# Attention entry of a fused attention and mixture-of-experts kernel: three waits for one, scores placed ahead of the ranks, and batch 0's copies on ScalarE

## The chip, the cores and the metric

One core of one Trainium2 chip. The metric is the device time of one launch in microseconds, as the median over runs of the same kernel. The profile is one further execution of it.

## The reference, cut to what matters

For x of 16 batches x 512 tokens x 128 features in float32 the result is x + attention(layernorm(x)) + experts(layernorm(x)):

```python
xn = (x - mean) / sqrt(var + 1e-5)
# attention: 16 heads of 8, causal
q, k, v = heads(xn @ Wq), heads(xn @ Wk), heads(xn @ Wv)
q, k = q / norm(q), k / norm(k)
o = softmax(where(causal, 8.0 * q @ k.T, -max)) @ v
attn = merge(o) @ Wo
# experts: 8 of 128 -> 512 -> 128, each token to its best two
probs = softmax(xn @ Wr.T)
top_v, top_i = top_k(probs, 2); top_v /= sum(top_v)
ffn = sum over e of (gelu(xn @ W1[e].T + b1[e]) @ W2[e].T + b2[e]) * weight_e
```

## The kernel before

**Stages.** Stage A (`stage_a`) goes through the 16 batches in pairs: LayerNorm on VectorE (DVE), transposes and the joint product with the router, q and k weights on TensorE (PE), squares, norms and copies on ScalarE (ACT), sums of squares on GpSimd (POOL). Then comes the entry of attention, which is what is changed. `attention` then runs batches 0 to 7, then the experts' tiles (`between`), then batches 8 to 15.

**The routing at the entry.** DVE picks the two best experts of each token in quarters (`select`, L1105); the last quarter is done after stage A. PE sums the picks (L985), DVE copies the sums (L1273, `totals`), PE multiplies them again (L992, L994, semaphore `counted`), and DVE works out from the counts where each expert's rows begin (L1280 to L1310). That gives `pad_at`: POOL fills the padding of the slots from a block of zeros with an indirect DMA (`pad_last_tiles`, L623, 128 rows of 8 KB; semaphore `padded`). PE gives each token its rank within its expert (L997 and L999, into PSUM bank 7, semaphore `placed`), DVE turns ranks into slot numbers (L1320 to L1328), clears the bank `ps_o` (L1331) and raises `routed`.

**A batch of attention.** It has 12 units of scores, each for three of the (side, half, head group) pieces of `PIECES`. PE computes a unit into one of two halves of six PSUM banks (`scores`, L892), ACT takes the exponential of the 1,536 columns (L812), POOL clears what is above the diagonal (`mask`, L664, one or two instructions a unit), and PE multiplies the probabilities with the values in ten chunks (`weigh`, L926) into `ps_o`. `scores` of unit k waits for the exponential of unit k-2; a chunk waits for the masks of all its units. Chunks 0 to 4 make the first half of a batch: DVE transposes it out of `ps_o` (`evacuate`, L1355), and chunk 5 waits for that (`o_evac`). Chunk 3 wants the masks up to unit 5, chunk 4 those up to unit 6, chunk 6 up to unit 8, chunk 7 up to unit 9.

**Preparing the next batch.** Between the units PE makes the next batch's four tiles of q, k and v (`project`, L870; each waits until the tile before it is out of bank 7, `proj_evac`). DVE scales q and k (L1222), copies the values out (L1229), splits q and k into two half precision parts (L1238, L1240) and doubles them (L1245, L1246, `dup_done`). SP then issues a DMA transpose of that tile into `qks` (`turn_qk`, L431). `scores(b, par, 0)` waits for all four transposes of its batch (`qk_turned`). Batch 0's four tiles are projected ahead of the routing (L978 on), each in a bank of its own. POOL's queue in batch 0 also carries eight indirect moves of token rows to their slots (`move`, L650). They stand between the masks of units 5 to 10, and ahead of the first of them, behind the mask of unit 5, POOL waits for `routed` and `padded`:

```python
order = [[], [], [], [], [], [0], [1, 2], [3], [4, 5], [6], [7], []]   # moves behind each unit's mask
```

Each engine carries out its own queue in the order of the program. In batch 0 PE's order is: scores 0 to 3, project(1,0), scores 4, weigh 0, scores 5, project(1,1), weigh 1, scores 6, weigh 2, scores 7, project(1,2), weigh 3, scores 8, project(1,3), scores 9, weigh 4, scores 10, weigh 5 and 6, scores 11, weigh 7, and then scores(1,0). DVE's order is share_values(0), the four `prepare` of batch 1, `pick_tiles`, `evacuate(0, 0)`, `divide`, share_values(1).

Of the kernel before, what the change touches and what calls it, by code (L numbers as in the profile page):

```python
# [29 lines left out]
def build(nc, x, Wq, Wk, Wv, Wo, Wr, W1, b1, W2_, b2, out):  # L30
# [68 lines left out]
    with ExitStack() as ctx:  # L99
# [154 lines left out]
        routed = sem("routed")  # L254
# [279 lines left out]
        def _(pool):  # L534
# [141 lines left out]
            def body(b, par, second=False, last=False):  # L676
# [3 lines left out]
                if known(b, 0):  # L680
                    pad_last_tiles()
                for k in range(UN):
                    mask(b, k)
                    if known(b, 0) and k == 5:
                        pool.wait_ge(routed, 1)
                        pool.wait_ge(padded, 16)
# [59 lines left out]
        def _(act):  # L746
# [28 lines left out]

            def step(i, par, j):
# [21 lines left out]
            stage_a(act, step)  # L798
            for s in range(2):
                squares(NB // 2 - 1, 1, s)  # L800
            for i in range(NB // 2 - 3, NB // 2):
                roots(i)
# [31 lines left out]
        def _(pe):  # L834
# [35 lines left out]
            def project(b, i):  # L870
# [4 lines left out]
                if not known(b, 0):  # L875
                    if i == 0 and known(b, 1):
                        pe.wait_ge(routed, 1)
# [48 lines left out]
            def weigh(b, par, c):  # L926
# [3 lines left out]
                if c == 0:  # L930
                    pe.wait_ge(proj_evac, TB * (b + 1))
                    if known(b, 0):
                        pe.wait_ge(routed, 1)
# [47 lines left out]

            pe.wait_ge(selected, T // ST)
# [13 lines left out]
            mm.then_inc(counted, 1)  # L996
            pe.matmul(ps_pc, before[:], flat_both, start=True, stop=False)  # L997
# [4 lines left out]
            pe.wait_ge(bt_ready, 1)  # L1002
            pe.wait_ge(proj_evac, TB)

            def body(b, par, second=False, last=False):
# [3 lines left out]
                fresh = known(b, 0) or known(b, HALF)  # L1009
                for k in range(UN):  # L1010
                    scores(b, par, k)
                    if k == 1 and not last and not known(b, 0):
# [3 lines left out]
                    elif k == 3:  # L1016
                        if not fresh:
                            weigh(b - 1, 1 - par, 9)
                        if not last:
                            project(b + 1, 0 if known(b, 0) else 1)  # L1020
                    elif k == 4:
                        weigh(b, par, 0)
                    elif k == 5:
                        if not last:
                            project(b + 1, 1 if known(b, 0) else 2)
# [3 lines left out]
                    elif k == 7:  # L1029
                        if not last:  # L1030
                            project(b + 1, 2 if known(b, 0) else 3)
                        weigh(b, par, 3)
                    elif k == 8 and known(b, 0):
                        project(b + 1, 3)
# [4 lines left out]
                    elif k == 9:  # L1039
# [4 lines left out]
                        if not known(b, 0):  # L1044
                            out_project(b - 1, TB * (b + 1) if last else TB * (b + 2))
# [53 lines left out]
        def _(dve):  # L1099
# [110 lines left out]
            def unload(b, par, i, late=False):  # L1210
# [5 lines left out]
                if some(tile):  # L1216
# [6 lines left out]
                    .then_inc(qn_done, 1)  # L1223
                if some(CN * (b - 2)):
# [6 lines left out]
            def halve(b, i):  # L1231
# [3 lines left out]
                if some(b):  # L1235
# [5 lines left out]
                    .then_inc(lo_done, 1)  # L1241
                dve.wait_ge(lo_done, tile + 1)
# [24 lines left out]
            for c in range(TOPK):  # L1267
                select(T // ST - 1, c)
            dve.wait_ge(btr_done, 1)
            dve.tensor_copy(wexp[:, :, B1C:W2C], psum[:, 5, 0:E * MC].rearrange("p (e c) -> p e c", e=E))\  # L1270
                .then_inc(bt_ready, 1)
            dve.wait_ge(counted, 1)
# [316 lines left out]
```

## Time and profile before

| what | value |
|---|---|
| median of three runs | 680.27 us (679.78 to 681.35) |
| the profiled execution's own time | 680.41 us |
| its span | 678.7 us |
| mean granted clock of TensorE | 0.975 |
| PE busy | 615.8 us (91%) |
| DVE busy | 465.7 us (69%) |
| ACT busy | 449.9 us (66%) |
| POOL busy | 418.0 us (62%) |
| mean DMA rate | 132 GB/s |

The busy times are sums over one execution. They say that PE is the engine with the least idle time; where its idle time lies has to be read from the stretches. Times of the timeline and of the windows are microseconds from the start of the span. A row of the timeline gives start, duration, engine, line, operation and names, and in square brackets how long the engine had been idle and what the profile holds responsible.

### The profile page before, as it was taken

How to read it: one execution, taken by the hardware profiler on the slowest of the kernel's cores; microseconds unless marked ns; L12 is line 12 of the kernel's file. 1: busy time of each engine (PE TensorE's matmuls, PEld its weight loads, DVE VectorE, ACT ScalarE, POOL GpSimd, SP SyncE). 2: the span in 40 equal slices, each digit the busy share in tenths (PEclk: the TensorE clock that was granted, in tenths of full speed). 3: DMA queues.
4: the chain of work that ended last, by engine and by line, in shares of the span. 5: the costliest groups of instructions: out<-in, count | busy, mean ns of one | idle time of the engine just before them, and what ended most of it. 6: DMA issues, size and time to landing. Idle time of an engine off the chain costs nothing. (4 is left out here: it accounts for less than half of the span.)

```text
span 678.7 us, 21454 instructions
## 1 busy us (share of the span) xinstructions
PE 615.8 (91%) x7417; PEld 411.7 (61%) x7417; DVE 465.7 (69%) x1312; ACT 449.9 (66%) x689; POOL 418.0 (62%) x584
## 2 busy tenths in 40 slices
PE   2877558999999999999999999999999999999965
PEld 2755323444444438999999999999984444444423
DVE  7799986766676776445545446777566687878826
ACT  3999546888888884444444444444449888888854
POOL 6355627778777787775600027677737777677771
PEclk9899968999999999999999999999999999999989
DMA  5997685655445578855432335444536375556621
GB/s 160 297 288 228 185 248 111 109 108 104 115 115 118 125 126 199 206 143 143 108 88 71 73 88 120 112 115 118 120 78 104 84 137 116 121 124 139 122 68 32
DMA packets 186592, 89.36 MB, mean 132 GB/s; under 512 B 115456, under 2 KB 176032, under 8 KB 186400
## 3 DMA queue, kind: packets, MB, share of 16 engines
q1 hardware_dynamic: 178192, 70.70, 44.7%
q0 software_dynamic: 8336, 17.84, 9.8%
q8 instruction: 36, 0.59, 0.4%
q14 instruction: 28, 0.23, 0.1%
HBM read 30.17 MB, written 32.24 MB: 92 GB/s over the span
## 5 line engine op out<-in xcount | busy, mean ns | idle before, releaser
L812 ACT ACTIVATE prob<-psum 128x1536 f32<-128x1536 f32 x192 | 267.2, 1453 | 64.0 <-PE psum L922 62.2
L822 ACT ACTIVATE prob<-psum,prob 128x256 f32<-128x256 f32 x284 | 117.5, 471 | 132.2 <-PE psum L1062 129.3
L648 POOL DMA_INDIRECT rows<-slot_y,idx x128 | 130.4, 1019 | 46.1 <-issue 27.2
L650 POOL DMA_INDIRECT slot_x<-rows,slots x128 | 128.2, 1001 | 36.1 <-issue 30.4
L954 PE MATMUL psum<-prob,v 128*18 128x448 f32 (+3 forms) x2048 | 137.9, 388 | 8.6 <-POOL prob L664 8.6
L664 POOL TENSOR_SCALAR_AFFINE_SELECT prob<-prob 128x384 f32<-128x384 f32 (+2 forms) x224 | 104.8, 477 | 62.6 <-ACT prob L812 60.5
L1074 PEld LDWEIGHTS psum<-prob 128*128 128x128 f32 x1136 | 137.8, 192 | 3.6
L1074 PE MATMUL psum<-prob 128*128 128x128 f32 x1136 | 138.1, 275 | 0.0
L1062 PE MATMUL psum<-xs,prob 128*128 128x256 f32 x568 | 134.8, 380 | 0.6 <-DVE xs L1468 0.4
L1062 PEld LDWEIGHTS psum<-xs,prob 128*128 128x128 f32 x568 | 102.5, 190 | 12.4 <-DVE xs L1468 0.6
L954 PEld LDWEIGHTS psum<-prob,v 128*18 128x18 f32 x2048 | 48.8, 98 | 97.0 <-issue 75.9
L922 PE MATMUL psum<-qks 32*128 32x192 f16 (+3 forms) x1024 | 74.2, 276 | 2.5 <-ACT prob L812 2.4
L1475 DVE TENSOR_TENSOR xs<-psum,prob 128x256 f32<-128x256 f32 x71 | 30.1, 425 | 52.5 <-PE psum L1074 52.5
L882 PE MATMUL psum<-wall,xt 128*128 128x384 f32 x128 | 58.5, 541 | 3.6 <-issue 3.1
L1452 DVE COPY prob<-wexp 128x516 f32 x71 | 31.4, 443 | 38.0 <-ACT prob L822 34.6
L922 PEld LDWEIGHTS psum<-qks 32*128 32x128 f16 x1024 | 22.1, 92 | 42.4 <-ACT prob L812 17.4
L1460 DVE COPY prob<-wexp 128x640 f32 x71 | 35.8, 505 | 14.8 <-DVE xs L1475 14.5
L1397 DVE SCALAR_TENSOR_TENSOR acc<-rows,gate,acc 128x128 f32<-128x128 f32 (+1 forms) x128 | 42.7, 398 | 1.4 <-DVE acc L1381 0.8
L633 POOL COPY idx<-slots 128x8 int32 (+1 forms) x16 | 3.7, 231 | 63.8 <-PE psum L1074 63.6
L1240 DVE TENSOR_TENSOR dup<-qn,dup 128x256 f16<-128x256 f32 x64 | 36.3, 567 | 2.2
L1222 DVE TENSOR_TENSOR qn<-psum,rnb 128x256 f32<-128x256 f32 x36 | 14.8, 412 | 31.1 <-PE psum L882 31.0
L845 PE MATMUL psum<-wall,xts 128*128 128x264 f32 x128 | 32.3, 399 | 4.2 <-ACT logits L767 4.2
(159 smaller groups left out, 661.3 us busy)
## 6 DMA issues: line engine op xcount, KB each, us to landing
slot_y<-xs SPq DMA_DIRECT2D x71, 128.0 KB
xs<-in_L_attn_x SPq DMA_DIRECT2D x16, 256.0 KB, 4.1
prob<-in_L_ffn_W SPq DMA_DIRECT2D x16, 256.0 KB, 3.6
xn_rows<-prob SPq DMA_DIRECT2D x16, 256.0 KB, 2.7
xn_cols<-xts SPq DMA_DIRECT2D x16, 256.0 KB, 3.0
xt<-xn_cols SPq DMA_DIRECT2D x16, 256.0 KB
rows<-xn_rows SPq DMA_DIRECT2D x16, 256.0 KB, 3.5
out<-acc SPq DMA_DIRECT2D x15, 256.0 KB
```

What stands on the lines that cost most here:

```text
L648: pool.indirect_dma_start(rows[:, j, c, t, :], None, done, where).then_inc(moved[j], 16)
L650: pool.indirect_dma_start(slot_x, where, halves_of_rows[:, j, 0, t, :], None).then_inc(moved[j], 16)
L664: pool.affine_select(out=p, in_=p, compare_op=ALU.is_ge, fill=0.0, base=HP, pattern=[[0, n], [0, 2], [1, HP]], channel_multiplier=-1).then ...
L812: act.activation(prob[:, KEPT[k], :], score[k % 2], ACT.Exp, scale=SCALE / UP ** 2)\
L822: act.activation(hs[:, s, c, :], psum[:, 2 * s + c // 2, (c % 2) * FT:(c % 2 + 1) * FT], ACT.Gelu, bias=ws[:, s, B1C + c:B1C + c + 1]).the ...
L882: pe.matmul(bank[:, 0:3 * D], xt[:, t * P:(t + 1) * P], wall[:, E:WEND], start=True, stop=True)\
L922: mm = pe.matmul(s[:, j * N + col:j * N + col + cols], keys, queries(qks[g:g + 32, par, 0, slab], kt, first, cols), start=True, stop=True)
L954: mm = pe.matmul(queries(ps_o[32 * g:32 * g + VW], kt, first, cols), pairs[par][:, kt * H // 2 + QH * o + g, odd:odd + VW], prob[:, KEPT[u ...
L1062: mm = pe.matmul(psum[:, 2 * s + c // 2, (c % 2) * FT:(c % 2 + 1) * FT], ws[:, s, c * P:(c + 1) * P], xgt[:, s, :], start=True, stop=True)
L1074: mm = pe.matmul(psum[:, 4 + s, j * D:(j + 1) * D], hs[:, s, c, j * P:(j + 1) * P], ws[:, s, W2C + c * D:W2C + (c + 1) * D], start=(c == 0 ...
L1240: dve.tensor_tensor(dup[:, t, :, :, 3 * DH:4 * DH], whole_qk, dup[:, t, :, :, 0:DH], ALU.subtract)\
L1397: dve.scalar_tensor_tensor(out=a, in0=r, scalar=gate[:, c, at(TB * m + t)], in1=a, op0=ALU.mult, op1=ALU.add).then_inc(combined, 1)
```

## The change

- `routed` is split. DVE raises `counts_read` behind L1280 and `ranks_read` behind L1321. In batch 0 weigh(0) waits for `counts_read`, and project(1,0) for `ranks_read`. POOL's moves still wait for `routed`. The clearing of `ps_o` is gone.
- PE computes unit 0 of batch 0's scores ahead of the wait for `selected` and the first sums, and units 1 and 2 between `counted` and the ranks' product (L997, L999).
- Behind that PE's order in batch 0 is: scores 3, weigh 0, scores 4, project(1,0), scores 5, weigh 1, scores 6, weigh 2, scores 7, weigh 3, scores 8, project(1,1), scores 9, weigh 4, project(1,2), scores 10, weigh 5 and 6, scores 11, project(1,3), weigh 7, scores(1,0).
- DVE moves `evacuate(0, 0)` from behind the four tiles of batch 1 to between the second and the third, and share_values(0) from behind the slots to ahead of the sums.
- ACT copies batch 0's values out of PSUM and doubles the halves of its four tiles, in place of DVE. Its last six square roots are put around that: batches 10 and 11 ahead of the last squares, batches 12 and 13 behind tiles 0 and 1, 14 and 15 at the end.
- POOL's `pad_last_tiles` goes from ahead of mask 0 to behind mask 1.

```diff
@@ -251,7 +251,7 @@
         r_step, counted, totals_read, placed = sems("r_step counted totals_read placed")
-        routed = sem("routed")
+        routed, counts_read, ranks_read = sems("routed counts_read ranks_read")
         residue_ready, later_ready = sems("residue_ready later_ready")
@@ -677,10 +677,10 @@
               pool.wait_ge(y_out[s], 16 * ((FFN_TILES + 1 - s) // 2))
-      if known(b, 0):
-          pad_last_tiles()
       for k in range(UN):
           mask(b, k)
+          if known(b, 0) and k == 1:
+              pad_last_tiles()
           if known(b, 0) and k == 5:
@@ -772,6 +772,11 @@
+
+  def root(b):
+      act.wait_ge(ss_ready, b + 1)
+      act.activation(norms[:, TB * b:TB * (b + 1), :], sums[:, b % 2], ACT.Sqrt, scale=1.0 / UP ** 2)\
+          .then_inc(norms_ready, 1)
@@ -796,10 +801,27 @@
   stage_a(act, step)
+  roots(NB // 2 - 3)
   for s in range(2):
       squares(NB // 2 - 1, 1, s)
-  for i in range(NB // 2 - 3, NB // 2):
-      roots(i)
+
+  def share_first(t):
+
+      act.wait_ge(qn_done, t + 1)
+      to = v[:, 0, t * H:(t + 1) * H, 0:DH].rearrange("p (m j) d -> p j m d", j=2)
+      act.copy(to, psum[:, t, 2 * D:3 * D].rearrange("p (j m d) -> p j m d", j=2, d=DH)).then_inc(proj_evac, 1)
+      act.wait_ge(lo_done, t + 1)
+      q_to = dup[:, t, 0].rearrange("p h (c d) -> p h c d", d=DH)
+      k_to = dup[:, t, 1].rearrange("p h (c d) -> p h c d", d=DH)
+      act.copy(q_to[:, :, 1:3, :], q_to[:, :, ::-3, :])
+      act.copy(k_to[:, :, 1:3, :], k_to[:, :, ::3, :]).then_inc(dup_done, 1)
+  act.wait_ge(made, 3)
+  for t in range(TB):
+      share_first(t)
+      if t < 2:
+          root(NB - 4 + t)
+  for b in range(NB - 2, NB):
+      root(b)
@@ -874,7 +896,7 @@
           if i == 0 and known(b, 1):
-              pe.wait_ge(routed, 1)
+              pe.wait_ge(ranks_read, 1)
           if i == 0 and some(b - 2):
@@ -930,7 +952,7 @@
           if known(b, 0):
-              pe.wait_ge(routed, 1)
+              pe.wait_ge(counts_read, 1)
       if c in (0, 5) and some(2 * b + o):
@@ -979,6 +1001,10 @@
+  pe.wait_ge(bt_ready, 1)
+  pe.wait_ge(proj_evac, TB)
+  scores(0, 0, 0)
+
@@ -994,22 +1020,47 @@
   mm.then_inc(counted, 1)
+  scores(0, 0, 1)
+  scores(0, 0, 2)
   pe.matmul(ps_pc, before[:], flat_both, start=True, stop=False)
...
   mm.then_inc(placed, 1)
-  pe.wait_ge(bt_ready, 1)
-  pe.wait_ge(proj_evac, TB)
+
+  def first_batch():
+
+      for k in range(3, UN):
+          scores(0, 0, k)
+          if k == 3:
+              weigh(0, 0, 0)
+          elif k == 4:
+              project(1, 0)
+          elif k in (5, 6, 7):
+              weigh(0, 0, k - 4)
+          elif k == 8:
+              project(1, 1)
+          elif k == 9:
+              weigh(0, 0, 4)
+              project(1, 2)
+          elif k == 10:
+              weigh(0, 0, 5)
+              weigh(0, 0, 6)
+          else:
+              project(1, 3)
+              weigh(0, 0, 7)
...
       fresh = known(b, 0) or known(b, HALF)
+      if known(b, 0):
+          first_batch()
+          return
       for k in range(UN):
           scores(b, par, k)
-          if k == 1 and not last and not known(b, 0):
+          if k == 1 and not last:
               project(b + 1, 0)
@@ -1017,21 +1068,19 @@
               if not last:
-                  project(b + 1, 0 if known(b, 0) else 1)
+                  project(b + 1, 1)
           elif k == 4:
...
               if not last:
-                  project(b + 1, 1 if known(b, 0) else 2)
+                  project(b + 1, 2)
               weigh(b, par, 1)
...
               if not last:
-                  project(b + 1, 2 if known(b, 0) else 3)
+                  project(b + 1, 3)
               weigh(b, par, 3)
-          elif k == 8 and known(b, 0):
-              project(b + 1, 3)
           elif k == 8 and known(b, 1):
@@ -1041,8 +1090,7 @@
                   pe.wait_ge(plan_ready, 1)
-              if not known(b, 0):
-                  out_project(b - 1, TB * (b + 1) if last else TB * (b + 2))
+              out_project(b - 1, TB * (b + 1) if last else TB * (b + 2))
           elif k == 10:
@@ -1221,6 +1269,8 @@
           .then_inc(qn_done, 1)
+      if known(b, 0):
+          return
       if some(CN * (b - 2)):
@@ -1239,6 +1289,10 @@
           .then_inc(lo_done, 1)
+      if known(b, 0):
+          return
+      if known(b, 1) and i == 0:
+          dve.wait_ge(dup_done, TB)
       dve.wait_ge(lo_done, tile + 1)
@@ -1264,11 +1318,12 @@
       prepare(0, 0, t)
-  for c in range(TOPK):
-      select(T // ST - 1, c)
   dve.wait_ge(btr_done, 1)
...
       .then_inc(bt_ready, 1)
+  for c in range(TOPK):
+      select(T // ST - 1, c)
+  share_values(0, 0)
   dve.wait_ge(counted, 1)
@@ -1278,6 +1333,7 @@
   stepped(dve.tensor_copy(counts[:], ps_o[:, 0:2 * E].rearrange("p (c e) -> p c e", c=2)))
+  dve.sem_inc(counts_read, 1)
   dve.tensor_copy(cnti[:, 0], counts[:, 0])
@@ -1319,6 +1375,7 @@
   stepped(dve.tensor_tensor(at_rank, ranks, of_halves(begins[:, 0:2]), ALU.add))
+  dve.sem_inc(ranks_read, 1)
   stepped(dve.tensor_tensor(ahead, ahead, of_halves(jumps[:]), ALU.mult))
@@ -1328,8 +1385,6 @@
-  dve.memset(ps_o, 0.0).then_inc(r_step, 1)
-  dve.wait_ge(r_step, next_step())
   dve.sem_inc(routed, 1)
@@ -1400,8 +1455,6 @@
-      if known(b, 0):
-          share_values(0, 0)
       if not (second or known(b, HALF)):
@@ -1413,6 +1466,8 @@
           prepare(b + 1, 1 - par, 1, second)
+          if known(b, 0):
+              evacuate(0, 0)
           prepare(b + 1, 1 - par, 2, second)
@@ -1420,9 +1475,10 @@
           pick_tiles()
-      if known(b, 1):
-          write_plan()
-      evacuate(b, 0)
+      else:
+          if known(b, 1):
+              write_plan()
+          evacuate(b, 0)
       divide(b, 0)
```

## Rows read from the trace of the kernel before

**Rows 1.** Busy time by stretch (us busy, number of instructions), then PE's granted clock, DMA

```profile
80.00:100.00 20.00, 8.34 (x101) 3.31 (x101) 17.29 (x53) 7.38 (x7) 8.63 (x13) 0.63 0.94 260
...
140.00:150.00 10.00, 9.70 (x148) 3.73 (x150) 8.00 (x22) 8.96 (x7) 8.36 (x13) 1.00 0.60 119
```

**Rows 2.** Timeline of PE at the entry and through batch 0

```profile
86.50 0.61 PE L985 MATMUL psum<-ones,both 128*128 128x128 f16 x4 [9.62 <-DVE gap L1135]
...
90.17 1.06 PE L906 MATMUL psum<-barred,identh 128*128 128x512 f16 x2
...
92.20 0.61 PE L906 MATMUL psum<-barred,identh 128*128 128x512 f16 x2
...
98.66 1.62 PE L882 MATMUL psum<-wall,xt 128*128 128x384 f32 x2 [3.11 <-issue]
...
112.94 1.06 PE L943 MATMUL psum<-prob,xts 128*18 128x64 f32 x32 [2.47 <-DVE turn L1355]
113.77 1.93 PE L954 MATMUL psum<-prob,v 128*18 128x448 f32 x16
...
116.10 1.06 PE L954 MATMUL psum<-prob,v 128*18 128x448 f32 x16
117.09 0.60 PE L906 MATMUL psum<-barred,identh 128*128 128x512 f16 x2
...
119.55 0.91 PE L882 MATMUL psum<-wall,xt 128*128 128x384 f32 x2
```

**Rows 3.** Timeline of SP's issues at the entry

```profile
83.60 1.28 SPq L431 DMA_TRANSPOSE qks<-dup  x1
...
86.83 0.92 SPq L443 DMA_DIRECT2D acc<-in_L_attn_x  x1
```

**Rows 4.** DMA issues, 78 to 160 us; the last number is us from issue to landing

```profile
qks<-dup SPq DMA_TRANSPOSE x16, 3.6
acc<-in_L_attn_x SPq DMA_DIRECT2D x1, 0.5 KB, 11.8
slot_x<-acc,pad_at POOLq DMA_INDIRECT x1, 7.8
```

**Rows 5.** Timeline of DVE at the entry and through batch 0

```profile
81.18 0.21 DVE L1246 COPY dup<-dup 128x256 f16<-128x256 f16 x1
...
86.28 0.17 DVE L1135 TENSOR_TENSOR gap<-top 128x16 f32<-128x16 f32 x1
...
88.26 0.17 DVE L1280 COPY counts<-psum 128x16 f32<-128x16 f32 x1 [0.41 <-PE psum L994]
...
97.14 0.69 DVE L1328 TENSOR_REDUCE slots<-rows 128x64 int32<-128x512 f32 x1
...
108.86 0.42 DVE L1222 TENSOR_TENSOR qn<-psum,rnb 128x256 f32<-128x256 f32 x1 [0.48 <-PE psum L882]
...
110.83 0.21 DVE L1246 COPY dup<-dup 128x256 f16<-128x256 f16 x1
```

**Rows 6.** Timeline of ACT ahead of the entry

```profile
74.66 0.38 ACT L766 ACTIVATE prob<-psum 128x256 f32<-128x256 f32 x1
...
83.81 0.31 ACT L773 ACTIVATE norms<-rows 128x128 f32<-128x128 f32 x1 [2.29 <-POOL rows L601]
```

**Rows 7.** Timeline of POOL through batch 0

```profile
93.23 1.21 POOL L623 DMA_INDIRECT slot_x<-acc,pad_at  x1 [7.93 <-issue]
...
104.77 0.98 POOL L650 DMA_INDIRECT slot_x<-rows,slots  x1 [0.25 <-issue]
...
110.95 0.55 POOL L664 TENSOR_SCALAR_AFFINE_SELECT prob<-prob 128x384 f32<-128x384 f32 x1
...
113.92 0.74 POOL L664 TENSOR_SCALAR_AFFINE_SELECT prob<-prob 128x128 f32<-128x128 f32 x2
```

**Rows 8.** Short stretches in which PE's granted clock fell, columns as in rows 1

```profile
95.50:96.00 0.50, 0.05 (x6) 0.00 (x0) 0.47 (x2) 0.50 (x1) 0.32 (x1) 0.50 1.03 283
...
112.50:113.00 0.50, 0.06 (x4) 0.06 (x8) 0.47 (x2) 0.50 (x1) 0.20 (x2) 0.55 1.09 214
```

## The prediction, made before the changed kernel was run

> **What bounds the kernel now.** I read the busy time by stretch first [rows 1]. In attention PE is busy 9.7 of 10 us, so there a microsecond gained or lost on PE stays to the end. At the entry, 80 to 100 us, it is busy 8.34 of 20 us and at a mean clock of 0.63: that is what can be won. The timeline of PE names the waits [rows 2]: 9.62 us until the last picks are made, 3.11 us until `routed`, 2.47 us until `ps_o` is evacuated. Batch 1 begins with the L906 at 117.09. Behind it PE has no wait to speak of, so **the start of scores(1,0), and the clock at which it starts, decide the time**. The sum below is for that one moment.
>
> **Batch 0's copies.** DVE loses eight halves copies and four value copies, ACT gains twelve. At 0.38 us for a copy of a tile of twice that width [rows 6] ACT's are 4 x 3 x 0.38 = 4.6 us, and with four roots of 0.31 it is done by about 81 us; it has nothing else until the first scores. So this costs nothing, and the last `dup_done` comes at about 80 in place of 81.39 [rows 5]. But SP issues the fourth transpose of batch 0 at 83.60 [rows 3], over 2 us behind that copy: its queue of weight loads and transposes set it, not `dup_done`. It lands 3.6 us later [rows 4], at **87.2, before and after**. The gain is nil there. The last picks, ready at 86.45 [rows 5], should be ready some 2.4 us earlier.
>
> **Unit 0 ahead of the sums.** PE now stands at unit 0 until 87.2, with the sums behind it. The picks made early buy nothing. Unit 0 at half clock takes 92.20 - 90.17 = 2.03 us [rows 2], so the sums start at 89.25 where they started at 86.50: everything that hangs on the counts is **2.75 us later**. Counts at 88.26 + 2.75 = 91.0 [rows 5]. In return the first exponential starts near 89.3, 3 us earlier than before.
>
> **Padding.** It was issued 93.23 - 88.26 = 4.97 us behind the counts [rows 7, 5], so it is now issued at 96.0; mask 1 is done by then, so the new place in POOL's queue costs nothing, and would cost a mask's half microsecond. Its landing took 7.8 us [rows 4]; it shared the DMA engines with the load of `acc`, issued at 86.83 and landed 11.8 us later at 98.6 [rows 3, 4]. Of the 7.8, 5.4 us were shared. If half of that was lost the transfer alone is 5.1 us. It now starts when `acc` has at most 2.65 us left: 5.1 + 1.3 = 6.4 at most, and I take 6.2 us, bounds 5.1 and 7.8: landing at **102.2**, between 101.1 and 103.8. It landed at 101.0 before.
>
> **A rule beside that.** The Trainium skill (DMA: Bandwidth & Descriptors, section on the anatomy of one DMA on the SWDGE path) gives such a DMA as 2.0 us plus bytes over 436e3; for this 1.05 MB that is an estimate of 4.4 us. The trace has 7.8 us for it, under load, and here the trace is used. By the rule the padding would be no limit at all; that is the first rival.
>
> **POOL sets batch 0.** Behind mask 5 it waits for `routed` and `padded`. `routed` came at 97.83 [rows 5], so it now comes at 97.83 + 2.75 = 100.6, a floor. Mask 5 should be done at about 100.6 too, its exponential being some 4 us earlier. Call X the moment when POOL gets past these waits. Before, X = 104.77 - 0.25 = 104.52. From X to the end of mask 8 there are four moves and masks 6 to 8: 111.50 - 104.52 = 6.98 us [rows 7]; to the end of mask 9, 114.66 - 104.52 = 10.1 us. The order of the moves is not changed, so these stay. X after = 102.2, so POOL gains only 2.3 of the 4 us that ACT and PE gain. Mask 8 is done at 109.2, and weigh 6 waits for it.
>
> **The evacuation** goes between DVE's second and third tile, where it waits for weigh 4 (mask 6, about X + 2.3 = 104.5, so weigh 4 ends at about 105.5). DVE's tiles 2 and 3 are queued behind it, but their products on PE come later still, so it costs nothing, and the 2.47 us wait of weigh 5 [rows 2] goes. The cleared bank goes from DVE's queue: under a microsecond, beneath the padding.
>
> **Project(1,3) goes last.** It was issued three units earlier; now it stands behind weigh 6 and scores 11. So: weigh 6 from 109.2, 0.99 us at full clock (117.09 - 116.10), scores 11 0.32, the product 0.85: 111.4. Then DVE's chain, 108.86 to 111.04 = 2.2 us [rows 5]: 113.6. Then SP 0.1 and the landing 3.6 [rows 4]: scores(1,0) can start at **117.2**. Before, this chain had ended long before 117.09. PE itself would be ready at about 113.3, when weigh 7 is through: the new wait is some 4 us and takes the place of both old ones.
>
> **The clock.** The granted clock fell within the 2.5 us wait ahead of weigh 5 and, earlier, where PE had been busy for little of the time [rows 8, 2]. A 4 us wait drops it too. Units 0 and 1 of batch 1 then cost 2 x 2.03 in place of 119.55 - 117.09 = 2.46: **+1.6 us**, which before was not paid there. Ahead of weigh 6 PE is idle for about 1.9 us behind one of about 0.5. If the clock falls already there, weigh 6 takes 1.87 (113.77 to 115.64, the same product at half clock), and the product 1.55 (from 98.66 to the next product): with scores 11, +1.7 us on the chain. Rows 8 have it either way, so I take half, +0.85.
>
> **Sum.** 117.2 - 117.1 + 1.6 + 0.85 = **+2.5 us**. The profiled execution took 680.41 us around its span of 678.7, 0.14 over the median of 680.27; the difference is carried to the median: 682.8 us.
>
> **Rivals.**
> - *The padding is no limit* (20%). It lands within 5 us, the lower bound above, and X is set by `routed` and mask 5 at about 101.0. For it: the load of `acc` is nearly through when the padding starts. Against: 7.8 us measured. Then everything in the sum is 1.2 us earlier, weigh 6 stays at full clock: 116.0 - 117.1 + 1.6 = +0.5, 680.8 us: no change. The estimate from the Trainium skill's DMA: Bandwidth & Descriptors gives this case.
> - *Faster* (16%). The wait ahead of scores(1,0) is short enough for the clock to hold. Its place is the chain from project(1,3) to the transpose: with X at its floor of 100.7, the DVE chain at 1.7 us (without POOL in its way) and landing in 3.5, scores(1,0) starts at 100.7 + 7.0 + 2.2 + 1.7 + 0.1 + 3.5 = 115.2, and at full clock that is -1.9 us, 678.4. It decides from the point where X is under 101 and the granted clock is still 1 at scores(1,0). For it: PE and ACT really are 4 us ahead by unit 5. Against: a wait of 2.5 us already lost the clock.
> - *Much slower* (14%). The padding takes its 7.8 us although less stands beside it (+1.6), and the clock falls ahead of weigh 6 for certain (+0.85): +5.0 us, 685.3.
> - *The change does not do what it says* in one part: unit 0 is no sooner than the transposes let it be, and the copies on ACT free DVE for nothing. That is in the forecast. Were SP to issue earlier all the same, X would have its floor some 2 us earlier; that is held in the faster case.
>
> **How the numbers follow.** The forecast holds 50%, with the much slower case beside it 64% slower; 20% no change; 16% faster. Both signs have a case, but the slower ones hold most. A measurement of this kernel tells about 0.2%, 1.4 us, from no change. The range goes from 678.7, where most of the faster case is still inside, to 685.3. The forecast's own range is 681.7 to 684.
>
> **What would show it.** Right: scores(0,0,0) starts at 87.2 with L985 behind it at 89.3; counts at 91.0; the padding issued at 96.0; the first move at 102 to 102.5; weigh 6 waits for L664; PE idle for about 4 us ahead of scores(1,0), released by the transpose `qks<-dup`, at 117 to 118, and the granted clock at 0.5 behind it; the stretches from 140 us on as before, only shifted. Wrong: L985 ahead of 88; the first move ahead of 101; scores(1,0) ahead of 116, or with the clock at 1; a batch of attention that takes another time than before; or a difference that arises behind 125 us.

## The result and the profile after

The changed kernel takes **683.22 us** (median of nine runs, 681.89 to 685.43) against 679.78 us for the kernel before on the same chip (nine runs): a ratio of **1.0052 [1.0037, 1.0067]**, slower by 3.4 us. The profiled execution took 681.89 us around a span of 680.1 us, at a mean granted clock of 0.974. A second set of executions gave the same kernel 1.0038 [1.0023, 1.0054], so a difference of 0.1 or 0.2% between two kernels below is not to be relied on.

The timeline of PE after (start, duration, engine, line, operation, shapes and count; in brackets the idle time before and its releaser) answers to [rows 2]. L928, L935 and L944 are the scores, L965 and L976 `weigh`, L904 `project`, L1011 to L1020 the sums, L1025 and L1027 the ranks.

```profile
76.51 0.24 PE L1002 MATMUL psum<-identf,b1n 32*128 32x32 f32 x1
86.57 1.01 PE L928 MATMUL psum<-barred,identh 128*128 128x512 f16 x2 [9.82 <-DMA qks<-dup]
...
88.62 0.61 PE L1011 MATMUL psum<-ones,both 128*128 128x128 f16 x4
...
97.69 1.06 PE L976 MATMUL psum<-prob,v 128*18 128x448 f32 x16 [0.43 <-POOL prob L664]
...
101.31 0.39 PE L944 MATMUL psum<-qks 32*128 32x448 f16 x6
103.39 0.91 PE L904 MATMUL psum<-wall,xt 128*128 128x384 f32 x2 [1.69 <-DVE v L1279]
...
107.18 0.64 PE L965 MATMUL psum<-prob,xts 128*18 128x64 f32 x32 [0.39 <-DVE turn L1410]
108.69 1.06 PE L976 MATMUL psum<-prob,v 128*18 128x448 f32 x16 [0.86 <-POOL prob L664]
...
110.00 0.91 PE L904 MATMUL psum<-wall,xt 128*128 128x384 f32 x2
111.78 1.06 PE L976 MATMUL psum<-prob,v 128*18 128x448 f32 x16 [0.86 <-POOL prob L664]
116.37 1.01 PE L928 MATMUL psum<-barred,identh 128*128 128x512 f16 x2 [3.53 <-issue]
...
120.49 1.65 PE L904 MATMUL psum<-wall,xt 128*128 128x384 f32 x2
...
139.75 0.60 PE L928 MATMUL psum<-barred,identh 128*128 128x512 f16 x2
...
159.12 0.60 PE L928 MATMUL psum<-barred,identh 128*128 128x512 f16 x2
```

The same view of the kernel before, at the places to compare with (the last product of stage A, unit 8 of batch 0, and the first products of batches 2 and 3):

```profile
76.64 0.24 PE L980 MATMUL psum<-identf,b1n 32*128 32x32 f32 x1
...
107.59 0.39 PE L922 MATMUL psum<-qks 32*128 32x448 f16 x6
...
137.01 0.60 PE L906 MATMUL psum<-barred,identh 128*128 128x512 f16 x2
...
156.38 0.60 PE L906 MATMUL psum<-barred,identh 128*128 128x512 f16 x2
```

The 3.11 us wait for `routed` and the 2.47 us wait for the evacuation are gone [rows 2]. In their place stand several waits of 0.4 to 1.7 us and one of 3.53 us, ahead of scores(1,0). That one ends with L928 at 116.37, 0.72 us *earlier* than the 117.09 of before. But batch 2, at 139.75, starts 2.74 us *later* than the 137.01 of before. The loss arises within batch 1, in 23.38 us where it was 19.92. From there each batch takes what it took: 159.12 against 156.38 for the start of batch 3, 19.37 us both times. In all fourteen traces (before, after and twelve experiments) batches 3 to 6 take 19.35 to 19.37 us each; batch 7 with the experts behind it takes 273.9 to 274.9, and from batch 8 on single executions differ, between 18.6 and 22.2 us a batch. The windows (columns as in [rows 1]) say why:

```profile
80.00:100.00 20.00, 12.21 (x185) 4.68 (x186) 14.87 (x48) 12.08 (x15) 5.74 (x10) 0.66 0.93 255
...
115.00:116.00 1.00, 0.00 (x0) 0.00 (x0) 0.96 (x4) 0.00 (x0) 0.15 (x1) 0.85 0.94 189
116.00:120.00 4.00, 3.63 (x71) 1.46 (x72) 1.14 (x2) 1.45 (x1) 0.00 (x0) 0.50 0.22 66
120.00:125.00 5.00, 5.00 (x37) 1.36 (x33) 0.84 (x3) 2.90 (x2) 3.05 (x5) 0.50 0.08 26
125.00:126.00 1.00, 1.00 (x14) 0.33 (x12) 0.87 (x4) 0.89 (x1) 0.00 (x0) 0.53 0.00 0
126.00:130.00 4.00, 4.00 (x68) 1.66 (x64) 2.88 (x10) 2.85 (x3) 2.05 (x3) 1.00 0.62 148
```

At the entry PE is busy 12.21 us of 20 in place of 8.34 [rows 1], so the change does what it says. Then PE stands still, its granted clock goes from 1 to 0.50 (1.2 GHz) between 115 and 116, and nearly 10 us of back-to-back work, 116.4 to 125.9, runs at half speed. Before, the half clock of that part lay from 112.5 [rows 8] to 116, and scores(1,0) began at full clock:

```profile
113.00:116.00 3.00, 3.00 (x54) 1.44 (x54) 2.89 (x6) 0.16 (x1) 2.81 (x5) 0.51 0.73 171
116.00:117.00 1.00, 1.00 (x22) 0.37 (x16) 0.07 (x1) 0.78 (x1) 0.83 (x2) 1.00 0.21 66
```

Three views tell how the late start comes about. DVE, with rows that answer to [rows 5]:

```profile
85.31 0.17 DVE L1183 TENSOR_TENSOR gap<-top 128x16 f32<-128x16 f32 x1
...
90.37 0.17 DVE L1335 COPY counts<-psum 128x16 f32<-128x16 f32 x1 [0.42 <-PE psum L1020]
...
110.95 0.42 DVE L1270 TENSOR_TENSOR qn<-psum,rnb 128x256 f32<-128x256 f32 x1 [1.64 <-PE psum L904]
...
112.78 0.21 DVE L1300 COPY dup<-dup 128x256 f16<-128x256 f16 x1
```

POOL, answering to [rows 7]:

```profile
94.92 1.21 POOL L623 DMA_INDIRECT slot_x<-acc,pad_at  x1 [0.70 <-DVE pad_at L1366]
...
102.21 0.98 POOL L650 DMA_INDIRECT slot_x<-rows,slots  x1 [2.25 <-ACT prob L834]
...
108.08 0.55 POOL L664 TENSOR_SCALAR_AFFINE_SELECT prob<-prob 128x384 f32<-128x384 f32 x1
```

SP's issues, and the DMA issues from 78 to 160 us (the last number is us from issue to landing), answering to [rows 3, 4]:

```profile
113.05 1.23 SPq L431 DMA_TRANSPOSE qks<-dup  x1
```

```profile
acc<-in_L_attn_x SPq DMA_DIRECT2D x1, 0.5 KB, 12.5
slot_x<-acc,pad_at POOLq DMA_INDIRECT x1, 6.5
```

The last product of project(1,3) feeds DVE at 110.95, the halves are doubled by 112.99, SP issues the transpose at 113.05, and 3.3 us later, when it has landed, scores(1,0) starts at 116.37. (The profile writes "issue" beside this wait; that it is the transpose follows from SP's issue, from its landing some 3.1 us later, and from e1 and e2 below.) PE had run out of work at 112.84.

### The profile page after: what moved, and what is told of

It reads as the page before. It is cut to its first block and busy times, and to the rows that moved or that the text cites. A ratio compares the mean times of both kernels' runs of the same rounds, so it can differ in the third digit from the quotient of the medians.

```text
span 680.1 us, 21457 instructions
## 1 busy us (share of the span) xinstructions
PE 616.8 (91%) x7417; PEld 410.9 (60%) x7417; DVE 465.9 (68%) x1299; ACT 452.8 (67%) x701; POOL 415.7 (61%) x584
## 5 line engine op out<-in xcount | busy, mean ns | idle before, releaser
L976 PE MATMUL psum<-prob,v 128*18 128x448 f32 (+3 forms) x2048 | 137.4, 387 | 10.7 <-POOL prob L664 10.7
L1110 PEld LDWEIGHTS psum<-xs,prob 128*128 128x128 f32 x568 | 102.5, 190 | 12.7 <-issue 1.3
L976 PEld LDWEIGHTS psum<-prob,v 128*18 128x18 f32 x2048 | 48.5, 98 | 98.8 <-issue 76.6
L944 PE MATMUL psum<-qks 32*128 32x192 f16 (+3 forms) x1024 | 74.4, 277 | 1.5 <-ACT prob L834 1.4
L904 PE MATMUL psum<-wall,xt 128*128 128x384 f32 x128 | 58.5, 541 | 2.2 <-DVE v L1279 1.7
L944 PEld LDWEIGHTS psum<-qks 32*128 32x128 f16 x1024 | 22.1, 93 | 42.1 <-ACT prob L834 18.4
```

The lines of the kernel that those rows point to most:

```text
L904: pe.matmul(bank[:, 0:3 * D], xt[:, t * P:(t + 1) * P], wall[:, E:WEND], start=True, stop=True)\
L944: mm = pe.matmul(s[:, j * N + col:j * N + col + cols], keys, queries(qks[g:g + 32, par, 0, slab], kt, first, cols), start=True, stop=True)
L976: mm = pe.matmul(queries(ps_o[32 * g:32 * g + VW], kt, first, cols), pairs[par][:, kt * H // 2 + QH * o + g, odd:odd + VW], prob[:, KEPT[u ...
L1110: mm = pe.matmul(psum[:, 2 * s + c // 2, (c % 2) * FT:(c % 2 + 1) * FT], ws[:, s, c * P:(c + 1) * P], xgt[:, s, :], start=True, stop=True)
```

## The experiments

Two theories had to be told apart: the **clock** behind the new wait, and the **order** of the queues (project(1,3) last, unit 0 ahead of the sums). In the table A is the start of the small product of `b1n`, the last of stage A (76.51 in the timeline above). Stage A itself ends up to 1 us sooner or later between executions, so entries are compared by their distance from A. Medians and ratios are against the kernel before on the same chip; the ratio with its interval is worked out over all executions and can differ from the quotient of the two medians by up to 0.1%. The fillers of some kernels are products into a bank that the next unit of scores starts anew; they change nothing that is computed.

| kernel | median (before's), us | ratio | wait, clock at scores(1,0) | batch 2 − A | batch 3 − A |
|---|---|---|---|---|---|
| before | | 1 | none, 1 | 60.37 | 79.74 |
| after | 683.22 (679.78) | 1.0052 [1.0037, 1.0067] | 3.53, half | 63.24 | 82.61 |
| e5, after again | 682.98 (680.03) | 1.0038 [1.0023, 1.0054] | 3.49, half | 63.65 | 83.02 |
| e1, fillers | 682.52 (680.83) | 1.0027 [1.0011, 1.0043] | filled, 1 | 59.98 | 80.41 |
| e2, project(1,3) sooner | 682.89 (680.83) | 1.0030 [1.0016, 1.0045] | 1.78, half | 62.40 | 81.77 |
| e3, unit 0 behind the sums | 685.92 (680.83) | 1.0069 [1.0051, 1.0087] | 4.06, half | 63.80 | 83.18 |
| e4, copies on DVE | 682.53 (680.83) | 1.0032 [1.0019, 1.0045] | 3.55, half | 63.43 | 82.81 |
| e6, e2 and fillers | 682.24 (680.03) | 1.0037 [1.0019, 1.0055] | filled, 1 | 60.32 | 80.82 |
| e7, before with the split waits | 679.30 (680.03) | 0.9988 [0.9974, 1.0003] | none, half for 0.3 us | 60.27 | 79.64 |
| e8, new order, old entry | 683.73 (680.03) | 1.0065 [1.0052, 1.0077] | 3.50, half | 63.06 | 82.43 |
| e9, e2 and short fillers | 681.52 (679.80) | 1.0024 [1.0007, 1.0041] | 1.50, 1 | 59.89 | 80.26 |
| e10, e7 and fillers | 680.98 (679.80) | 1.0019 [1.0003, 1.0034] | none, 1 | 60.23 | 80.82 |
| e11, e9 with the old entry | 681.58 (679.80) | 1.0027 [1.0010, 1.0043] | filled, 1 | 57.88 | 78.30 |
| e12, new entry, old order | 683.50 (679.80) | 1.0057 [1.0035, 1.0080] | none, 1 | 63.75 | 83.12 |

**Fillers in the wait (e1).**

```diff
 # PE, ahead of scores(1, 0)'s waits for qk_turned
+ pe.wait_ge(exp_done, 11)
+ for _ in range(15):
+     pe.matmul(score[0][:, 0:N], identh[:], filler, start=True, stop=True)
```

> The changed kernel with 15 filler products (128 x 512, float16) of PE between weigh 7 and the wait for batch 1's transposes, into the bank of scores that unit 0 of batch 1 writes next. Theory (the loss is the clock that the wait of 3.5 us drops): scores(1,0) still starts at about 116.4 us, but at a granted clock of 1; batch 1 takes 19.9 us in place of 23.4, batch 2 starts at about 136.3, and the median falls by about 3.5 us to 679.7, level with the kernel before. Rival (the loss is the later counts, padding and moves): nothing that the filler touches, 683 us as before the edit.

Windows of e1_filler, columns as above:

```profile
116.00:120.00 4.00, 3.85 (x80) 1.61 (x77) 2.23 (x5) 1.22 (x1) 0.28 (x1) 1.00 0.48 119
120.00:125.00 5.00, 4.70 (x61) 1.70 (x65) 3.16 (x8) 4.60 (x5) 3.69 (x6) 1.00 0.10 30
```

Its timeline of PE:

```profile
117.45 0.59 PE L933 MATMUL psum<-barred,identh 128*128 128x512 f16 x2 [0.15 <-issue]
...
137.35 0.60 PE L933 MATMUL psum<-barred,identh 128*128 128x512 f16 x2
```

The clock stays at 1. scores(1,0) starts at 117.45 and batch 2 at 137.35, 19.90 us later, where the changed kernel took 23.38. So in the trace the 3.5 us that batch 1 lost are the clock. The mean granted clock says that this holds beyond the trace: it is 0.979 over the twelve executions of e1 and 0.972 over the nine of the changed kernel. The time follows only in part. The theory said level with the kernel before, its rival no change; the median gives back 0.11 to 0.25%, by which of the two measurements of the changed kernel it is set beside, and the intervals overlap. That lies between the two and decides for neither. One part of what is missing can be seen, a wait ahead of batch 3 that the kernels without fillers lack. With it, e1 is 2.2 us ahead of the changed kernel at batch 3, not 3.5:

```profile
157.78 0.60 PE L933 MATMUL psum<-barred,identh 128*128 128x512 f16 x2 [0.98 <-DMA qks<-dup]
```

**project(1,3) sooner (e2).** The product goes from behind scores 11 to ahead of weigh 5.

```diff
-                        weigh(0, 0, 5)
+                        project(1, 3)
+                        weigh(0, 0, 5)
                         weigh(0, 0, 6)
                     else:
-                        project(1, 3)
                         weigh(0, 0, 7)
```

> The changed kernel with project(1,3) raised from behind scores 11 to between scores 10 and weigh 5. Theory (the wait for the fourth transpose and the clock it drops): the product at about 107.7, its halves at 110.5, landing at about 114.1; scores(1,0) starts there behind a wait of about 1.3 us and the clock holds; batch 2 starts at about 134.0 in place of 139.75, and the median is 5 to 6 us under the changed kernel, about 677.5, which is 0.3 to 0.4 per cent under the kernel before. Rival (POOL's moves set the end of batch 0): weigh 7 and with it scores(1,0) move by under 1 us, 682 to 683 us.

PE's timeline and windows of e2_p3_sooner:

```profile
112.25 1.06 PE L976 MATMUL psum<-prob,v 128*18 128x448 f32 x16 [1.58 <-POOL prob L664]
115.09 1.01 PE L928 MATMUL psum<-barred,identh 128*128 128x512 f16 x2 [1.78 <-issue]
```

```profile
114.00:115.00 1.00, 0.00 (x0) 0.00 (x0) 0.95 (x3) 0.00 (x0) 0.92 (x1) 0.97 0.89 225
115.00:116.00 1.00, 0.91 (x2) 0.14 (x2) 0.97 (x2) 0.00 (x0) 0.62 (x2) 0.50 0.55 203
```

scores(1,0) is 1.3 us sooner and its wait half as long, and the clock falls all the same: batch 1 takes 23.63 us. What stands ahead of it is one wait of 1.58 us and one of 1.78, with only weigh 7 between. So shortening the wait is worth the 1 us or so by which the start moves and does not save the clock, which the theory had expected it to; the median stays where the rival put it.

**Unit 0 behind both sums (e3).**

```diff
-            scores(0, 0, 0)
             pe.wait_ge(selected, T // ST)
...
             mm.then_inc(counted, 1)
+            scores(0, 0, 0)
             scores(0, 0, 1)
```

> The changed kernel with unit 0 of batch 0's scores behind both sums in place of ahead of them. Theory: the sums start with the picks at about 85.6 in place of 88.6, counts at 87.4, padding issued at about 92, the first move at about 100 (set by mask 5 now, not by the slots), so scores(1,0) starts about 2 us sooner, at 114.4; but the wait for the fourth transpose stays near 3.5 us and the clock still falls: 681 to 681.5 us. Rival (the later counts are the whole loss): 680 us or less, level with the kernel before.

The rival, that the later counts are the whole loss, does not come about, nor does the gain of the theory. In e3_sums_first the counts come at 87.71, 2.66 us sooner, and the padding is still issued at 94.31:

```profile
94.31 1.21 POOL L623 DMA_INDIRECT slot_x<-acc,pad_at  x1 [0.63 <-issue]
```

`pad_at` itself was ready at 91.84; the padding stood in POOL's queue behind mask 1, which came later because its unit did. The first move is at 101.84, against 102.21. Meanwhile the product of project(1,3) falls to half clock (1.65 us where it took 0.91), the case that the forecast had half counted in. What was won at the counts is lost in the queue, and the kernel is the slowest of all. This says nothing on unit 0 with the padding in its old place; e12 comes back to that.

**Copies back on DVE (e4).** `share_first` is left out of ACT, which does its last four square roots in a row, and DVE's `prepare` of batch 0 is whole again, as in the kernel before.

> The changed kernel with batch 0's value and halves copies back on DVE, ACT keeping only the roots. Theory (these copies are hidden behind SP's queue and the transposes): the picks are ready some 2 us later, at about 87.5, still ahead of the end of unit 0 at 88.6; the transposes land as before at 86.6; no change, 682.7 to 683.7 us. Rival (DVE's relief brings the entry forward): the sums start 1 us or more later and the median is 684 us or more.

The last picks come at 86.58, 1.1 us later than in the changed kernel, and unit 0 ends behind them, at 89.2. The ratio is 1.0032: below the first interval of the changed kernel ([1.0037, 1.0067]), inside the second ([1.0023, 1.0054]), and its own interval overlaps both. The entry is the same (82.81 against 82.61 to batch 3). The copies are worth nothing that these runs can tell.

**The changed kernel once more (e5).** No edit.

> The changed kernel once more, beside the others of this set on one chip, as the measure for them. 1.005 of the kernel before, within 0.0015.

The same wait (3.49 us), the same half clock, batch 1 in 23.12 us. It serves as the second measure in the table.

**e2 with fillers (e6).** e2 and the 15 fillers of e1.

> Both edits at once: project(1,3) ahead of weigh 5, and 15 filler products ahead of the wait for batch 1's transposes. Theory (order and clock are two separate costs): scores(1,0) starts at about 115.1 us as with the product raised alone, and at a granted clock of 1, so batch 1 takes 19.9 us and batch 2 starts at about 135.0, some 2 us ahead of the kernel before: ratio to it about 0.997. Rival (something else than these two costs the time): ratio 1.002 or more.

The fillers held the clock, and ran to 117.29. But they did not use up what e2 had won: the fourth transpose, issued at 112.35, landed only at 117.09, 4.7 us later, where in e2 the same one (issued at 111.70) took 3.2. So scores(1,0) could not have started more than 0.2 us sooner without them, and the "1.4 us past the landing" in the expectation of e9 is a misreading. The last section comes back to this landing. The median falls on the rival's side, 1.0037, no faster than e1.

**The split waits alone (e7).** The kernel before, with these edits:

```diff
 # project(1, 0)
-                pe.wait_ge(routed, 1)
+                pe.wait_ge(ranks_read, 1)
 # weigh(0, 0, 0)
-                pe.wait_ge(routed, 1)
+                pe.wait_ge(counts_read, 1)
 # DVE, ahead of routed
-            dve.memset(ps_o, 0.0).then_inc(r_step, 1)
-            dve.wait_ge(r_step, next_step())
```

> The kernel before with one part of the change alone: routed split into counts_read and ranks_read for weigh 0 and project(1,0), the clearing of ps_o gone; the order of PE and DVE as before. Theory (the split wins at the entry and the change's new order gives it back): the 3.1 us wait ahead of project(1,0) shrinks to about 0.3, a new wait of project(1,1) for DVE's first tile comes to about 100.5; evacuate and with it weigh 5 some 1.7 to 2 us sooner, scores(1,0) at about 115.2 in place of 117.1: ratio 0.997. Rival (POOL's first move sets it anyway): 1.000.

PE's timeline of e7_split_alone:

```profile
100.03 1.06 PE L943 MATMUL psum<-prob,xts 128*18 128x64 f32 x32 [1.68 <-DVE xts L1260]
...
113.76 0.64 PE L943 MATMUL psum<-prob,xts 128*18 128x64 f32 x32 [2.46 <-DVE turn L1355]
```

The wait for `routed` turns into 1.68 us for DVE's copy of the values, and the 2.46 us wait for the evacuation stays, since DVE still goes through slots, four tiles and `pick_tiles` ahead of it. Batch 2 comes 60.27 us behind A, as before (60.37), and the ratio's interval holds 1. The theory of a gain (0.997) did not hold: splitting a wait moved PE to the next thing that the same engine owed it.

**New order with the old entry (e8).** Units 0 to 2 behind the ranks' product, the padding ahead of mask 0, and the rest as in the changed kernel.

```diff
+            mm.then_inc(placed, 1)
+            for k in range(3):
+                scores(0, 0, k)
```

> The changed kernel with units 0 to 2 back behind the ranks' product and the padding back ahead of mask 0; the new order of batch 0, the split and the copies on ACT stay. Theory (the order that puts project(1,3) last makes the loss, with any entry): counts at about 87.5, padding issued at about 92.5 and landed by 100.5, the first move at about 101.5 behind mask 5, scores(1,0) at about 116 behind a wait of 3.5 us or so and with the clock at half: ratio 1.003 to 1.005. Rival (unit 0 ahead of the sums makes it): 1.000 or less.

1.0065, against e7's 0.9988 with the old order. Both have the old entry, so the new order (with the copies, which e4 found neutral) costs 0.77% (4.4 us by the two medians). The traces show the same wait, 3.50 us, ahead of scores(1,0) at 116.03 and the half clock behind it; from A to batch 3 they differ by 2.8 us.

**Short fillers (e9).** e2 with 6 fillers ahead of weigh 7 and 7 ahead of scores(1,0).

> The changed kernel with project(1,3) ahead of weigh 5, and fillers fitted to the waits that were left: 6 products ahead of weigh 7 and 7 ahead of the wait for batch 1's transposes (15 in one place reached 1.4 us past the landing). Theory (the order and the clock are the two costs): the granted clock stays at 1 from unit 5 on, scores(1,0) starts at about 115.2 us, batch 2 at about 135.2, 1.8 us ahead of the kernel before: ratio to it 0.9975. Rival (a cost that neither touches): 1.002 or more.

They hold the clock and end ahead of the landing (1.50 us are left). Here too the fourth transpose lands late, 4.3 us behind its issue at 112.00. Counted from A, batch 2 is 0.48 us sooner than in the kernel before; at batch 3, behind a wait of 0.92 us, it is 0.52 us later, and the median is 0.24% slower, where the theory said 0.25% faster.

**Fillers beside the split alone (e10).** e7 with 6 fillers ahead of weigh 5.

> The kernel before with the split waits alone, and 6 filler products in the 2.5 us wait ahead of weigh 5. Theory (that wait costs the clock as well): weigh 5 to weigh 7 run at full clock in place of half, 1.5 to 2 us, and scores(1,0) starts at full clock: ratio about 0.9965 against 0.999 without the fillers. Rival (the clock falls or comes back by itself whatever the fillers do): 0.999.

The half clock of weigh 5 and 6 [rows 8] is gone, yet batch 2 comes 60.23 us behind A and no sooner. The fillers ran from 112.88 to 114.28 and held weigh 5 back by about 1.2 us: e7's wait ended at 113.76 in an execution whose stage A was 0.67 us later, so the like moment here is 113.1, and weigh 5 starts at 114.28. What the clock gave, the fillers took, and the theory (0.9965) failed on that. Then comes the wait of 1.16 us at batch 3. 1.0019 [1.0003, 1.0034]: worse than e7, if anything.

**e9 with the old entry (e11).** The entry of e8 in e9.

> As the first of this set (project(1,3) ahead of weigh 5, 6 and 7 fillers), with units 0 to 2 behind the ranks' product and the padding ahead of mask 0. Theory (where the first three units stand makes little of the time): within 0.001 of the first of this set. Rival (the scores ahead of the sums cost something that the trace hides): 0.002 or more below it.

The fastest entry of all in its trace, batch 2 2.5 us and batch 3 1.4 us sooner than in the kernel before, and the median is still 0.27% slower. The trace of one execution and the median part here, and no run explains it (see the end). The theory of the expectation, within 0.001 of e9, held.

**New entry with the old order (e12).** The changed kernel, but with PE's projects and DVE's evacuation where they were before.

```diff
 # PE, batch 0
+                    if k in (3, 5, 7, 8):
+                        project(1, (3, 5, 7, 8).index(k))
+                    if 4 <= k <= 7:
+                        weigh(0, 0, k - 4)
 # DVE, batch 0: evacuate(0, 0) behind tile 4 and pick_tiles()
```

> The changed kernel with batch 0 in the order of the kernel before, on PE and on DVE: the four tiles of batch 1 behind units 3, 5, 7 and 8, the evacuation behind the fourth tile and pick_tiles. The split waits, the three units ahead and the copies on ACT stay. Theory (the new order makes the loss): the wait ahead of scores(1,0) is gone, the wait of weigh 5 for the evacuation is back, scores(1,0) starts at about 117.7 and at full clock: ratio 1.001 to 1.002, against 1.004 to 1.005 for the changed kernel. Rival (the loss is in the other parts): 1.004 or more.

PE's timeline of e12_old_order:

```profile
103.35 1.65 PE L904 MATMUL psum<-wall,xt 128*128 128x384 f32 x2 [4.99 <-DVE v L1273]
...
116.24 1.06 PE L965 MATMUL psum<-prob,xts 128*18 128x64 f32 x32 [2.12 <-DVE turn L1404]
...
120.36 0.60 PE L928 MATMUL psum<-barred,identh 128*128 128x512 f16 x2
```

I had taken the order alone for the loss, and that falls: with the old order scores(1,0) starts at full clock, but at 120.36. Unit 0 ahead of the sums makes the slots late, DVE comes to batch 1's first tile only behind them, and PE stands 4.99 us ahead of project(1,1) and works at half clock from 103 to 109, and again for weigh 5. The median, 1.0057, is the rival's. The four kernels make a square:

| | old order | new order |
|---|---|---|
| old entry | e7 0.9988 | e8 1.0065 |
| new entry | e12 1.0057 | after 1.0052 and 1.0038 |

Against e7 the new order alone costs 0.77%, the new entry alone 0.69%, and both together 0.50 to 0.64%. They are not additive: in each corner another wait is the last one, and the new order hides the late slots beneath the wait that it makes itself. (e7 has DVE's copies, the other three ACT's; by e4 that makes no difference here.)

## Why the prediction was right, point by point

- **What bounds it** held in the trace: the difference is made by the start of scores(1,0) and its clock, and batches 2 to 6 take what they took.
- **Batch 0's copies** cost nothing, as said, and SP's queue set the transposes: unit 0 started at 86.57 (forecast 87.2). The last picks came 0.97 us sooner (85.48), not 2.4, and the last halves were doubled at 82.28, not at about 80: later than before (81.39), and hidden only because SP issued that transpose at 83.23. DVE's casts and differences of batch 0 were slower beside POOL's sums of squares, one line of DVE and one of POOL in the changed kernel:

```profile
74.91 1.28 DVE L1288 CAST dup<-qn 128x256 f16<-128x256 f32 x1
```

```profile
74.77 1.27 POOL L594 TENSOR_TENSOR rows<-prob 128x512 f32<-128x512 f32 x1 [0.17 <-POOL rows L601]
```

  The same cast takes 0.28 us where POOL stands still; here it ends 0.15 us behind POOL's product. The Trainium skill (SBUF — State Buffer, section on who interferes with whom) says that a cast can take the port pair that DVE shares with GpSimd, and that whoever is second is blocked for the other's whole instruction. The trace agrees. It did no harm, because PE was waiting for the transposes.
- **Unit 0 ahead of the sums**: counts 2.11 us later (90.37 against 88.26), forecast 2.75.
- **Padding**: issued at 94.92 (forecast 96.0) and 6.5 us to land (taken as 6.2 between 5.1 and 7.8). The estimate of 4.4 us from the Trainium skill's DMA: Bandwidth & Descriptors, SWDGE section, was too low here too, though the load of `acc` had by then only about 4 us left (86.46 + 12.5 = 98.96). So the first rival, padding no limit, did not come about. Yet the slots (101.3, forecast 100.6) came within 0.2 us of the padding (101.4), so by itself a faster padding would have bought next to nothing. (The forecast took 97.83 for `routed` before; that is the end of the last slots [rows 5], and `routed` came behind the clearing of `ps_o`, at 98.5. The clearing is gone in the changed kernel, so the floor of 100.6 was rightly built on 97.83.)
- **POOL sets batch 0**: first move at 102.21 (forecast 102 to 102.5), mask 8 done at 108.63 (forecast 109.2). The 1.69 us wait of project(1,1) for DVE's first tile was not foreseen; it lies beneath POOL's chain.
- **The evacuation** costs 0.39 us in place of 2.47.
- **project(1,3) last**: the new wait is 3.53 us where some 4 were forecast. The chain is right link by link: product at 110.00, halves at 112.99 (113.6), scores(1,0) at 116.37 (117.2). e2 and e8 show it from two sides.
- **The clock** is the term that was mis-sized. 1.6 us for units 0 and 1 of batch 1 is what those two cost (116.37 to 120.49 is 4.12 us in place of 2.46). But the clock stayed low for 10 us, not for two units: project, weigh 8 and the next units were in it as well, and batch 1 lost 3.46 us. The other half of the term, 0.85 us for a clock that falls ahead of weigh 6, was not paid: weigh 6 took 0.99 us (L976 at 108.69).
- **Luck.** With its 0.85 us the forecast had scores(1,0) 0.95 us later than before; it came 0.72 us sooner, 1.7 us off. Behind it 1.6 us were forecast and 3.46 paid, 1.9 us off the other way. The two errors cancel, +2.5 us forecast and +2.74 at batch 2 in the trace, and nothing in the forecast made them cancel.
- **The medians** moved by 3.4 us, and by 2.95 us in the second measurement. The 0.2 to 0.7 us beyond the trace are within what single executions of one kernel differ by: from the start of batch 3 to the end of the span it is 521.0 us for the changed kernel and 523.8 us for the same one again (e5).

Where the gain went can be read from PE's timelines of the two kernels: at unit 8 (L944 at 101.31, which was L922 at 107.59) PE is 6.3 us ahead, at weigh 7 (111.78 and 116.10, [rows 2]) 4.3 us, at scores(1,0) 0.72 us, and at batch 2 it is 2.74 us behind. Of the 6.3 us, 1.7 are not a gain but two products of `project` put off (0.85 us each), done by weigh 7. The wait of project(1,1) and POOL's moves and masks took the rest of the first part, the last producer of batch 1, put at the end, the second, and the clock the third.

## What to carry to other kernels

Ahead of moving the last producer of a stage's input down a queue, add up the whole chain behind it (here product, scaling, halves, transpose, landing: 6.4 us) and compare it with the work that is left; what does not fit becomes a wait, and the wait is paid a second time in the clock behind it. Ahead of splitting a wait, look which engine owes the next thing: in e7 it was the same one, and nothing was gained. Measure the parts of a two-part change as a square of four kernels, since each can hide the other's cost.

## What was not expected, and what stays open

- The half clock outlasted its cause. PE was busy without a gap from 116.4 to 125.9 us and stayed at 0.50 nearly all that time, while before it was back at 1 after 3.5 us (112.5 to 116, [rows 8]), and in e12 5.6 us behind the start of work at 103.35. What decides between these was not tried.
- The clock fell behind waits of 1.58 and 1.78 us (e2), where it held through a wait of 1.50 us with six fillers ahead of weigh 7 (e9).
- All five kernels with fillers (e1, e6, e9, e10, e11) wait 0.9 to 1.2 us for a transpose ahead of batch 3, and none without them does. In the traces of e1, e6, e9 and e11 the last transpose of batch 3 lands 4.6 to 4.7 us behind its issue; in those of the nine kernels without fillers it lands 3.05 to 3.15 us behind it (a few completions are missing from the traces). What differs beside it is a packet of 16 KB in DMA queue q8, which the profile calls `instruction`: it starts 2.2 to 2.3 us behind the issue of the transpose in those four, and 2.5 to 3.0 us in the nine. In batches 1 to 3 of the fourteen traces such a packet starts 0.3 to 2.4 us behind the issue of a transpose 28 times, and all 28 transposes take 3.9 to 4.7 us, the late ones of batch 1 in e6 and e9 among them. So fillers may cost by moving these packets onto a transpose that is waited for. That is a coincidence in time and not shown as the cause: no run moved the packets alone, transposes with no such packet beside them took 3.05 to 4.4 us, and where it starts later, 2.5 to 3.0 us behind the issue, some land after 3.05 us and others, e10's (packet at 2.8, landing at 4.8) among them, after 4.8 to 5.1.
- The kernels with fillers are 0.19 to 0.37% slower by their medians, though their entries are between 1.4 us sooner and 1.1 us later than before at batch 3. From these differences the medians lie 0.1 to 3.2 us higher than the entries would give. For the kernels without fillers the same comparison gives 1.4 us lower to 1.7 us higher, so only e11, with its 3.2 us, stands out. Where that time goes no trace shows: the rest of the span is 521.9 to 527.0 us in the kernels with fillers and 520.9 to 524.0 us in the others, and one execution of each cannot settle it. So the clock's share of the loss, 3.5 us in the trace, is shown in the medians only in part, and no version here beats the kernel before beyond its interval; e7 comes nearest.
